# Reordering the fill and the tail of a two-layer conditioned residual kernel on four engine queues

## Time and profile before

| | before |
|---|---|
| time, median of 3 runs | 888.69 us (887.59 to 889.04) |
| the profiled execution | 889.04 us, span 887.2 us |
| PE busy | 850.8 us, 96% of the span |
| DVE / POOL / ACT busy | 707.8 / 631.2 / 483.2 us |
| granted TensorE clock, mean | 0.984 of full speed |

### The profile page before, as it was taken

One profiled execution on the slowest core, in us unless ns is written; L12 is line 12 of the kernel. 1 busy time (PEld: TensorE's weight loads), 2 busy tenths in 40 slices (PEclk: granted clock), 3 DMA queues, 4 the chain that ended last, 5 costly groups with the idle time before them and its releaser, 6 DMA issues.

```text
span 887.2 us, 19766 instructions
## 1 busy us (share of the span) xinstructions
PE 850.8 (96%) x7474; PEld 769.7 (87%) x7474; DVE 707.8 (80%) x1099; ACT 483.2 (54%) x851; POOL 631.2 (71%) x766
## 2 busy tenths in 40 slices
PE   5997899999999999999999999999999999999997
PEld 5854787989999898999899898989899898999986
DVE  3588798789897877779898877789898877879642
ACT  3566555465646546465546546455555646464531
POOL 2367799768877766778877766768878776856562
PEclk9897999999999999999999999999999999999999
DMA  8972233425243342424343342424434342322110
GB/s 288 418 239 58 66 85 108 123 51 150 72 143 90 85 114 72 119 67 141 81 143 90 84 115 57 117 69 136 101 108 102 85 112 51 102 66 79 48 49 25
DMA packets 104367, 95.56 MB, mean 108 GB/s; under 512 B 72880, under 2 KB 78160, under 8 KB 102608
## 3 DMA queue, kind: packets, MB, share of 16 engines
q1 hardware_dynamic: 95056, 69.26, 27.4%
q0 software_dynamic: 4608, 16.78, 6.9%
q10 hardware_dynamic: 4608, 8.25, 2.8%
HBM read 69.60 MB, written 8.40 MB: 88 GB/s over the span
## 4 chain that ended last, share of the span: by engine, by line
PE 67%; DVE 15%; POOL 5%; issue 5%; ACT 4%; DMA 2%; ACTq 0%; DVEq 0%; POOLq 0%; SPq 0%
PE acc L392 30%; PE tok L392 24%; PE att L392 6%; PE xp L545 4%; PE xp L392 2%; DVE op0l L1370 2%; DVE Wkl L1170 2%; DMA kb<-in_kb 1%; DVE SE L1307 1%; POOL op0l L1678 1%; DVE SE L1298 1%; DVE xb L1332 1%; DVE small L1334 1%; DVE ytmp L1364 1%; DVE small L1303 1%
## 5 line engine op out<-in xcount | busy, mean ns | idle before, releaser
L1678 POOL TENSOR_TENSOR op1l<-ytmp,op1h 128x512 fp32r<-128x512 f32 x64 | 86.3, 1349 | 15.8 <-ACT op1h L892 15.3
L1624 POOL TENSOR_TENSOR xlo<-xraw,xhi 128x512 fp32r<-128x512 f32 x31 | 42.7, 1377 | 50.3 <-ACT xhi L787 50.2
L392 PE MATMUL acc<-op0h,W1xh 128*128 128x256 f32 x256 | 75.7, 296 | 2.7 <-DVE op0l L1350 2.7
L392 PE MATMUL acc<-op1h,W1th 128*128 128x256 f32 x256 | 75.4, 294 | 0.0
L392 PE MATMUL acc<-op1h,W1hh 128*128 128x256 f32 x256 | 73.7, 288 | 0.0
L392 PE MATMUL acc<-op0h,W1sh 128*128 128x256 f32 x256 | 73.7, 288 | 0.0
L892 ACT CAST op1h<-ytmp 128x512 fp32r<-128x512 f32 x64 | 39.8, 621 | 60.9 <-DVE ytmp L1364 60.9
L392 PE MATMUL acc<-op1h,W1tl 128*128 128x256 f32 x256 | 72.8, 284 | 0.0
L392 PE MATMUL acc<-op1l,W1th 128*128 128x256 f32 x256 | 72.8, 284 | 0.0
L392 PE MATMUL acc<-op0h,W1sl 128*128 128x256 f32 x256 | 72.4, 283 | 0.0
L392 PE MATMUL acc<-op0l,W1sh 128*128 128x256 f32 x256 | 72.4, 283 | 0.0
(11 more groups left out here) (270 smaller groups left out, 3190.6 us busy)
## 6 DMA issues: line engine op xcount, KB each, us to landing
xsq<-in_x SPq DMA_DIRECT2D x32, 256.0 KB
xb<-in_x SPq DMA_DIRECT2D x32, 256.0 KB, 3.0
out<-xb SPq DMA_DIRECT2D x32, 256.0 KB, 2.2
BD<-q SPq DMA_DIRECT2D x124, 64.0 KB, 2.1
BD<-v SPq DMA_DIRECT2D x124, 64.0 KB
xraw<-in_xT SPq DMA_DIRECT2D x30, 256.0 KB, 3.0
ring<-in_k_wT ACTq DMA_DIRECT2D x6, 256.0 KB, 3.7
dmb<-dm_rows SPq DMA_DIRECT2D x6, 256.0 KB, 3.8
```

Source lines behind the costliest of these rows:

```text
L392: return e.matmul(o, a, b, start=start, stop=True, skip_group_check=True)
L1624: e.tensor_tensor(xlo[:, :, :], (xraw1 if g == 1 else xraw)[:, :, :], xhi[:, :, :].bitcast(F32), ALU.subtract).then_inc(s["xlo"], 1)
L1678: e.tensor_tensor(op[slot]["l"][:, :, half(g)], four(ytmp[YT[n, g][0]]), op[slot]["h"][:, :, half(g)].bitcast(F32), ALU.subtract).then_inc ...
```

## The change

No instruction is added or removed; the order changes on all five queues, in the first pair (preamble and k = 1) and in the last two iterations (k = 15 and k = 16). SP issues `load_tok(2)` later. PE at k = 15 issues `a_T(31)`, `out_proj(31)`, `x_T(30)` and `x_T(31)` one part of W2 earlier. ACT at k = 15 makes `prod_hi(30, "t")` before `u_copy(30)`. DVE at k = 15 does `x_one(31)` before `last_stats(28)`. POOL moves `add_ob(2)` from the preamble into k = 1, moves `root2(1)`, the pieces of the W1h split and of the W2 split against each other, and at the end moves `root3(29)` ahead of `affine(31)`, `add_be(30)` and `add_be(31)` ahead of `prod_lo(30, "s")`, and `add_ob(31)` ahead of `prod_lo(30, "t")`.

```diff
--- before.py
+++ after.py
@@ -335,7 +335,6 @@
             blocks_q(1)
             e.wait_ge(s["m1"], 1)
             e.dma_start(stg["a"][:, :, :], A["int_w1"][3]).then_inc(s["c_rn"], 16)
-            load_tok(2)
             e.dma_start(raw["2"][:, :, :], A["int_w2"]).then_inc(s["c_r2"], 16)
             e.wait_ge(s["tq"], 1)
             e.dma_start(beint[:, :], A["int_be"].partition_broadcast(128)).then_inc(s["c_rp"], 16)
@@ -347,6 +346,7 @@
             blocks_q(2)
             e.wait_ge(s["stt"], 8)
             e.dma_start(rp[:, :], A["rows_p"]).then_inc(s["c_rp"], 16)
+            load_tok(2)
             load_tok(3)
             for k in range(1, NT + 1):
                 a, b, pa, pb = 2 * k, 2 * k + 1, 2 * k - 2, 2 * k - 1
@@ -716,22 +716,23 @@
                     gains(a, "t")
                     u_T(a)
                 W2_part(pa, (0, 1))
+                if front and not more:
+                    a_T(b)
                 W2_part(pb, (0, 1))
                 if front and not more:
-                    a_T(b)
+                    out_proj(b)
+                    x_T(a)
                 W2_part(pa, (2, 3))
+                if front and not more:
+                    x_T(b)
                 if more:
                     a_T(b)
                     scores(a + 2)
-                elif front:
-                    out_proj(b)
-                    x_T(a)
                 W2_part(pb, (2, 3))
                 if more:
                     out_proj(b)
                     x_T(a)
                 elif front:
-                    x_T(b)
                     id_rows(k, True)
             assert seen == list(XP), [x for x in zip(seen, XP) if x[0] != x[1]][:3]
 
@@ -1104,14 +1105,14 @@
                     split_x(b + 2)
                     squares(b + 2)
                 if front:
+                    if not more:
+                        a_hi(b)
+                    prod_hi(a, "t")
                     if more:
-                        prod_hi(a, "t")
                         u_copy(a)
                         a_hi(b)
                     else:
-                        a_hi(b)
                         u_copy(a)
-                        prod_hi(a, "t")
                     if more:
                         sum_part(a + 2, "S", "Sc")
                     if more:
@@ -1539,10 +1540,9 @@
                     product(a, "t")
                 elif front:
                     a_lo(b)
+                    x_one(b)
                 last_stats(pa)
                 last_gain(pa)
-                if front and not more:
-                    x_one(b)
                 if more:
                     a_lo(b)
                     w_T(a + 2)
@@ -1716,7 +1716,6 @@
             affine(0)
             x_lo(3)
             bounds(3)
-            add_ob(2)
             root2(0)
             e.wait_ge(s["wh"], 1)
             e.wait_ge(s["Pm"], 3)
@@ -1741,15 +1740,16 @@
                 else:
                     prod_lo(pb, "t")
                     affine(pb)
-                    e.wait_ge(s["wh"], 3)
-                    split_lo(W1["h", "l"], raw["h"], W1["h", "h"], None, (0,))
+                    add_ob(a)
+                root2(pb)
                 if not front:
-                    root3(pb - 2)
-                root2(pb)
+                    add_be(pa)
+                    add_be(pb)
                 if mod_of(k):
                     mod_scale(*mod_of(k), (2, 3))
                 if k == 1:
-                    split_lo(W1["h", "l"], raw["h"], W1["h", "h"], None, (1,))
+                    e.wait_ge(s["wh"], 3)
+                    split_lo(W1["h", "l"], raw["h"], W1["h", "h"], None, (0,))
                 elif front:
                     add_ob(a)
                 prod_lo(pa, "s")
@@ -1758,26 +1758,22 @@
                     bounds(a + 2)
                 prod_lo(pb, "s")
                 if k == 1:
-                    split_lo(W1["h", "l"], raw["h"], W1["h", "h"], None, (2,))
+                    split_lo(W1["h", "l"], raw["h"], W1["h", "h"], None, (1,))
                 prod_lo(pa, "h")
                 if front:
                     root1(a)
                     gather(a)
                 prod_lo(pb, "h")
-                if not front:
-                    add_be(pa)
-                    add_be(pb)
                 if k == 1:
-                    split_lo(W1["h", "l"], raw["h"], W1["h", "h"], s["wlp"], (3,))
+                    split_lo(W1["h", "l"], raw["h"], W1["h", "h"], s["wlp"], (2, 3))
+                    e.wait_ge(s["wh"], 5)
+                    split_lo(WL["2", "l"], raw["2"], WL["2", "h"], None, (0,))
                 if front:
                     true_scale(b)
                     affine(a)
                     if k == 1:
-                        e.wait_ge(s["wh"], 5)
-                        split_lo(WL["2", "l"], raw["2"], WL["2", "h"], None, (0, 1))
+                        split_lo(WL["2", "l"], raw["2"], WL["2", "h"], s["wlp"], (1, 2, 3))
                     root2(a)
-                    if k == 1:
-                        split_lo(WL["2", "l"], raw["2"], WL["2", "h"], s["wlp"], (2, 3,))
                     if k == 1:
                         add_be(0)
                         add_be(1)
@@ -1786,11 +1782,8 @@
                     if more:
                         x_lo(b + 2)
                         bounds(b + 2)
-                    if more:
-                        add_ob(b)
+                    add_ob(b)
                     prod_lo(a, "t")
-                    if not more:
-                        add_ob(b)
                     gather(b)
                 if more:
                     true_scale(a + 2)
@@ -1801,6 +1794,8 @@
                     root1(b)
                     if more:
                         add_be(a)
+                    else:
+                        root3(pb)
 
 
 def kernel(**inp):
```

## The result

| | before | after |
|---|---|---|
| median | 888.18 us (887.59 to 889.04) | 895.36 us (894.71 to 897.03, 4 runs) |
| ratio | | 1.0079, 95% interval 1.0060 to 1.0097 |
| profiled execution | 889.04 us, span 887.2 | 892.25 us, span 890.4 |

The change makes the kernel slower by 7.2 us. The forecast was slower by 2.9 us, with a range that ended at 894.3: the direction held, the size did not. Four more executions of after on record, the profiled one among them, took 892.25 to 896.38 us.

What follows compares the result with a forecast made beforehand. PE, busy 96% of the span with next to no slack in the middle, bounds the kernel. Fill 1.8 plus tail 1.1 gives 2.9 us, on median 888.69 a forecast of 891.6; the 8 in 10 range is 887.9 to 894.3.

Steps and rivals of the forecast that it cites:

- no delay is made good in the middle: Steady middle, 140 to 835 us: PE has next to no slack, so a delay carried in at 140 us stays.
- W1h starts: Fill: the slid W1h pieces end at 125.71, so PE starts W1h 1.3 us later, near 125.8.
- Values wait: Fill: PE's values matmuls start at 134.4 to 134.5, their wait growing from 1.50 to 2.2 us.
- Silu's low part: Fill, DVE: second silu's low part ends at 140.8 to 141.3, PE wants it at 140.7; adds 0 to 0.6 us.
- The fill's term: Before 140 us: the fill loses 1.5 + 0.3 = 1.8 us, with ends of 0.8 and 2.9.
- the time of `root2(2)`: Fill, POOL: it ends at 136.0 to 137.0, middle 136.6, against 133.34 before, behind three W2 pieces.
- into the upper end only: Fill: POOL's back-to-back pieces block DVE's subtraction, making `true_scale(3)` 0.55 us later; counted only in the upper end.
- a rival with 0.22 and 1.5 us: Fill: the clock falls as well behind the new 2.2 us idle time, costing 1.5 us, 893.1 in all; chance 0.22.
- The tail's term: After 835 us: the tail loses 1.1 us, with ends of -0.5 and +1.8.
- `add_ob(31)`, taken at nothing: Tail, POOL: moving this add earlier costs nothing, since POOL was idle before it.
- the 0.53 us earlier: Tail, PE: with `a_T(31)` ahead of one W2 part, `out_proj(31)` comes at 841.85, 0.53 us earlier.
- the wait at W1t: Tail: `affine(31)` behind `root3(29)` starts at 852.9; t's low part ends near 857.3 against PE's arrival at 857: 0.3 us.

Runs made afterwards that it cites:

- its second profile: The changed kernel run and profiled once more, nothing altered; 895.43 us, ratio 1.0068 to before.
- fill_only: The kernel before with only the change's edits in the fill (SP's load, preamble, k = 1); 893.02 us, ratio 1.0038 to before.
- ts_early: The changed kernel with no W2 piece ahead of `true_scale(3)`, all four between `affine(2)` and `root2(2)`; 896.36 us, ratio 1.0070 to before.
- root2_mid: The changed kernel with `root2(2)` between the second and third W2 pieces; 892.37 us, ratio 1.0064 to before.
- w1h_slide: The changed kernel with W2 split as before; of the fill's changes, `add_ob(2)` in k = 1 and slid W1h pieces stay; 891.18 us, ratio 1.0039 to before.
- tail_ob_late: The kernel before with only the k = 15 and 16 changes, but `add_ob(31)` back behind `prod_lo(30, "t")`; 892.50 us, ratio 1.0026 to before.
- dve_first_held: The changed kernel with filler matmuls in PE's waits, POOL's last two W1h pieces waiting for DVE's subtraction; 892.81 us, ratio 1.0020 to before.
- tail_pe_held2: Before with filler and the tail's changes, but `root3(29)`, `add_be(30)` and `add_be(31)` in their old places; 886.34 us, ratio 0.9993 to before.
- the second set: The set that timed the changed kernel again beside each of its halves alone; the changed kernel took 895.43 us, ratio 1.0068 to before.
- the filled pair: Before and after, each with filler matmuls in PE's fill waits, timed in one set; 884.70 us (0.9955) and 890.68 us (1.0021).

## Why the prediction was wrong

Times after are moved by the 0.88 us by which its first mark comes earlier (121.01 against 121.89).

**What held.** That no delay is made good in the middle: it takes 687.1 us behind the longer fill and 687.3 behind before's. W1h starts: forecast 125.8, measured 125.7. Values wait over 2 us: 2.70. The first W2 matmul waits no longer for the split; `u_T(2)` is late for ACT's `pgb`. Silu's low part ends at 141.1, forecast 140.8 to 141.3, partly by luck: it began 0.3 us later than forecast and took 0.65 us, not up to 1.23. In the tail `a_T(31)` stands 0.70 us (forecast 0.84), the W1x wait is 1.10, over 1.06, and `affine(31)` stands behind `root3(29)`.

**The fill's term, 1.8 forecast, 2.4 measured.** The failed step is the time of `root2(2)`, which ended 0.9 us later than its forecast middle. Some 0.4 of it is the delay that I worked out as 0.55 us for DVE held by POOL and took "into the upper end only": `true_scale(3)` started at 127.5 and not at 127.1. The other 0.5 is the length of the W2 pieces. The Trainium skill ("SBUF — State Buffer", section "SBUF: two separate sides") has the port pair as an exclusive lock for a whole instruction: the trace agrees, and goes further, since the subtraction at 121.33 stayed blocked through three pieces back to back and ended at 126.58, 0.56 us after the last. Three W2 pieces took 4.68 us, 1.56 each, above my 1.28 to 1.48, so `root2(2)` ended at 137.5 against my middle of 136.6.

**The clock, left out of the forecast.** This is the step that weighs most. I had it as a rival with 0.22 and 1.5 us, 893.1 in all. It fell in all three profiles with the full fill of the change and no filler (after, its second profile, `fill_only`) and in three with part of it (`ts_early`, `root2_mid`, `w1h_slide`), stayed low for 6.8 us and cost 2.0 in after's order. With before's fill and no filler at this place it fell in one profile of four (`tail_ob_late`). I compared the new wait with the old ones by its length alone: 2.21 us fell, 1.50 did not. The runs show that this was the wrong test. `w1h_slide` fell at 134 us with no wait over 1.5 us in the 30 us before. The 2.2 us wait near 101 us stands in twelve profiles without filler there: the clock fell behind it in ten, and in two, `root2_mid` and `dve_first_held`, it did not. In `root2_mid` the wait ended at 100.59 and was followed by:

```profile
101.00:104.00 3.00, 3.00 (x44) 3.00 (x42) 2.13 (x4) 2.52 (x6) 2.92 (x3) 1.00 0.03 5
```

The length of one wait does not decide. How idle PE was over the neighbourhood may be the better test (in after, PE worked 1.30 us of the 4 before 134), which no run here settles, and chance has its part, as these two and `tail_pe_held2` show. The Trainium skill ("TensorE: Matmul & The Clock Gate", section "What's actually happening") says that the throttled state is the default and activity releases it; the trace agrees, as the low stretches at 102 us (before) and at 135 us (after) follow on PE's waits of 2.21 and 2.70 us.

**The tail's term, 1.1 forecast, 2.0 measured.** The first failed step is `add_ob(31)`, taken at nothing because "POOL was idle before it". POOL was idle, DVE was not: the add at 837.07 lies beside silu's low part (1.46 us for 0.69), which moves the product's end from 2.68 us behind `u_T(30)` to 3.06, and that is what `a_T(31)` waits for. So `out_proj(31)` came 5.32 us behind `u_T(30)` against 5.35 before, and the 0.53 us earlier that I had counted on is gone. W1x is 13.51 us behind `u_T(30)` instead of 12.10, 0.6 more than forecast; `affine(31)` began 16.87 us behind `u_T(30)` (855.04 - 838.17), forecast 15.87 (852.9 - 837.03), and the low part behind it took 1.72 us and not 1.3, so the wait at W1t is 0.61 for my 0.3. Of the 0.9 us that were missing, `add_ob(31)` is 0.4 and the wait at W1t 0.3; 0.2 on the way to W1x stay open.

**The sum.** 2.4 + 2.0 + 2.0 = 6.4 of the 7.2 us (6.7 in the second set), all three read from marks in traces. The rest is open: it lies in the range by which the middle differs between executions of one kernel, and the filled pair has an unplaced 1.5 of the same kind. The traces give no sign that the change makes the middle long more often: 10 of 24 of the stretches described at the end are long with before's fill, 14 of 36 with the changed one.

## What to carry to other kernels

An engine that is idle is not free to take an instruction: ask what stands beside it on the engine that shares its port, and what that one feeds. When a bound worked out from the rows speaks against a change, put it into the sum and not only into the range. Where PE is at 96% and has no slack, do not call the clock safe because a new wait is no longer than one that did no harm; filler matmuls in the waits are a cheap test, and here a gain of 0.45% to 0.48% on the kernel before.

## What the runs showed of the hardware

Beside POOL's 128x512 work DVE's subtraction ahead of `true_scale(3)` took 1.55, 2.79, 4.0 or 5.25 us, by how many more POOL instructions stood back to back behind the one that it began beside (`dve_first_held` none, before one, `w1h_slide` two, after three).

The middle has stretches of two lengths. From ACT's cast of tile 5's q to that of tile 7's, and likewise from 13 to 15 and from 21 to 23, takes 50.0 us (up to 50.3 in a few) or 50.9. In a long one, before, silu's low part goes as follows, and in a short one, after, as in the second fence:

```profile
184.34 1.85 DVE L1370 SCALAR_TENSOR_TENSOR op0l<-ytmp,op0h 128x512 fp32r<-128x512 f32 x1 [1.72 <-ACT op0h L907]
```

```profile
187.88 0.82 DVE L1371 SCALAR_TENSOR_TENSOR op0l<-ytmp,op0h 128x512 fp32r<-128x512 f32 x1 [1.48 <-ACT op0h L908]
```

After's first profile had three short ones (50.0 each) and its second three long ones (50.9 each): 2.7 of the 2.9 us between their middles. What decides it was not tried.
